# Attention and expert layer: stacked Q and K parts kept once in DRAM, reciprocals and statistics moved, top-2 late

## The reference

```
x = x + xattn(layernorm(x), ctx, ctx)     # 16 tiles of 128 rows, HD = 8 rows a head: 256 x 256 scores a head
x = x + ffn(layernorm(x))                 # gate: 2 of 8 experts a row, 256 -> 512 -> 256, silu(h0) * h1
qk = einsum('bdm,bdn->bmn', qh, kh) * 8 ** -0.5;  sm = softmax(qk);  ret = einsum('bmn,bcn->bcm', sm, vh)
```

## Time and profile before

| what | value |
|---|---|
| median of 3 runs | 544.45 us (544.16 to 548.63) |
| profiled execution | 544.45 us |
| its span | 542.7 us |
| TensorE, share of the span busy | 81% |
| VectorE | 52% |
| ScalarE | 42% |
| GpSimd | 40% |
| granted TensorE clock, mean | 0.898 |
| DMA in all | 69.91 MB, mean 129 GB/s |
| SyncE's DMA queue | 29698 packets, 41.37 MB |

### The profile page before, as it was taken

One profiled execution on the slowest core, in us unless ns is written; L12 is line 12 of the kernel. 1 busy time (PEld: TensorE's weight loads), 2 busy tenths in 40 slices (PEclk: granted clock), 3 DMA queues, 4 the chain that ended last, 5 costly groups with the idle time before them and its releaser, 6 DMA issues.

```text
span 542.7 us, 10122 instructions
## 1 busy us (share of the span) xinstructions
PE 439.4 (81%) x3150; PEld 228.9 (42%) x3151; DVE 283.7 (52%) x599; ACT 230.6 (42%) x456; POOL 216.0 (40%) x224
## 2 busy tenths in 40 slices
PE   0336789889897967999714899999999999999991
PEld 0301234234342423332312465665665665665660
DVE  7169887988888857964789122222222222222220
ACT  0302698686777764787400322222222222222220
POOL 3530703262626333333383134534444544544522
PEclk9955699898999997788955799999999999999996
DMA  5899547586776892537393022232232232232321
GB/s 183 200 302 280 167 118 197 168 229 185 217 211 187 245 276 92 200 103 248 109 383 105 30 40 39 42 54 39 40 56 39 42 55 39 41 56 39 41 38 19
DMA packets 45208, 69.91 MB, mean 129 GB/s; under 512 B 6887, under 2 KB 34200, under 8 KB 45176
## 3 DMA queue, kind: packets, MB, share of 16 engines
q1 hardware_dynamic: 29698, 41.37, 27.0%
q0 software_dynamic: 11424, 24.39, 19.8%
q10 hardware_dynamic: 4054, 3.72, 2.4%
HBM read 42.57 MB, written 26.58 MB: 127 GB/s over the span
## 4 chain that ended last, share of the span: by engine, by line
PE 53%; DMA 18%; DVE 13%; ACT 6%; SPq 6%; issue 2%; POOLq 0%; POOL 0%; DVEq 0%; ACTq 0%
PE max_ps L1379 25%; DMA den<-acc 7%; PE ring_ps L1389 6%; PE pv_ps L1389 6%; ACT pt L742 5%; PE pv_ps L1283 5%; DVE mx L888 5%; DMA acc<-pvs 4%; PE ring_ps L1362 3%; PE ring_ps L1266 3%; SPq L425 2%; DMA q_img<-qpart 2%; PE max_ps L1178 2%; PE ring_ps L1352 2%; SPq L371 2%
## 5 line engine op out<-in xcount | busy, mean ns | idle before, releaser
L888 DVE TENSOR_REDUCE mx<-max_ps 128x4 f32<-128x1024 f32 x128 | 150.3, 1216 | 29.8 <-PE max_ps L1178 29.5
L742 ACT ACTIVATE pt<-ring_ps 128x512 f32<-128x512 f32 x256 | 139.1, 598 | 48.5 <-PE ring_ps L1266 45.8
L1379 PE MATMUL max_ps<-w_sb,pt 128*128 x312 | 143.0, 602 | 0.9 <-ACT pt L813 0.9
L682 POOL DMA_INDIRECT out<-rb,sidx x39 | 62.1, 1591 | 119.3 <-DVE gidx L1126 55.4
L1150 DVE TENSOR_TENSOR pt<-pt,max_ps 128x512 f32<-128x512 f32 x39 | 26.8, 688 | 125.2 <-PE max_ps L1379 66.2
L1283 PE MATMUL pv_ps<-pt,w_sb 128*27 128x256 f32 (+2 forms) x1024 | 85.4, 419 | 1.4 <-ACT pt L742 0.6
L1178 PE MATMUL max_ps<-K,Q 48*128 48x256 bf16 x512 | 56.8, 306 | 33.1 <-DVE mx L888 24.7
L1379 PEld LDWEIGHTS max_ps<-w_sb,pt 128*128 128x128 f32 x312 | 57.2, 193 | 58.8 <-issue 58.8
L1266 PE MATMUL ring_ps<-Q,K 50*128 50x256 f16 x512 | 54.4, 294 | 14.2 <-ACT pt L742 12.9
L820 ACT ACTIVATE pt<-ring_ps 128x512 f32<-128x512 f32 x39 | 23.3, 597 | 71.5 <-PE ring_ps L1362 71.5
L674 POOL DMA_INDIRECT pt<-xrow,gidx x39 | 38.8, 996 | 28.5 <-issue 14.0
(11 more groups left out here) (161 smaller groups left out, 398.7 us busy)
## 6 DMA issues: line engine op xcount, KB each, us to landing
w_sb<-in_L_ffn_w_kernel POOLq DMA_DIRECT2D x16, 512.0 KB, 7.6
K<-k_img SPq DMA_DIRECT2D x16, 448.0 KB, 6.0
Q<-q_img SPq DMA_DIRECT2D x16, 448.0 KB, 7.2
q_img<-qpart SPq DMA_DIRECT2D x32, 192.0 KB, 3.9
k_img<-kpart SPq DMA_DIRECT2D x28, 192.0 KB, 3.8
wo_sb<-in_L_ffn_wo_kernel POOLq DMA_DIRECT2D x8, 512.0 KB, 9.2
acc<-pvs SPq DMA_DIRECT2D x7, 512.0 KB, 3.8
q_sb<-in_x SPq DMA_DIRECT2D x16, 128.0 KB, 4.8
```

Source lines behind the costliest of these rows:

```text
L682: g.indirect_dma_start(xacc, bass.IndirectOffsetOnAxis(ap=sidx[sl.par][:, 0:1], axis=0), y_sb[sl.par], None, compute_op=ALU.add).then_inc( ...
L742: a.activation(pt[:, (2 * i + h) % PTN, :, :], bank(key)[:, :, :], ACT.Exp, scale=SCALE).then_inc(ring_read, 1)
L888: v.tensor_reduce(mx[:, t % 2, :, :, p].rearrange("q mt h -> q h mt"), max_ps[n % 2][:, :, :, :], axis=AX.X, op=ALU.max).then_inc(max_read, 1)
L1379: last = nc.tensor.matmul(flat(max_ps[sl.par][:, bank_of]), lhsT=xT[sl.par][:, k * P:(k + 1) * P], rhs=weight(w, e, KC, k), start=(k == 0) ...
```

## The change

- `q_img` and `k_img` hold each part once. `store_stack` issues four DMAs a group. `load_qk` issues six: for each half of `K` 48 rows of 8 KB that read 24 rows twice, for each half and part of `Q` 24 rows of 8 KB that read 8 rows three times. The fills of the images go.
- All x tiles are loaded at the start, and their statistics and normalisations stand before the loop.
- `recip` moves from pair 2 to pair 6 of the odd tile, `rows_stats` from pair 4 to pair 7. In the odd tile SyncE does `store_stack` and `store_rows` before `store_rd` and `load_rb`.
- GpSimd splits Q before `residual_norm`; the weight loads w0 and half of wo move behind the residual 4. `x_last` is loaded in tile 12.
- The top-2 of tiles 0 to 7 is taken at once after the loop. The weights' share of `told` is made on VectorE after the token's, and its 32 matmuls (`slot_weights`) stand between the slots 0 and 1 of the experts.

```diff
-        q_img = nc.dram_tensor("q_img", [3, IMG, PAIRS * 2 * M], f16).ap()
-        k_img = nc.dram_tensor("k_img", [3, IMG, PAIRS * 2 * M], bf16).ap()
+        q_img = nc.dram_tensor("q_img", [3, 2, QPARTS, HD * PAIRS, 2 * M], f16).ap()
+        k_img = nc.dram_tensor("k_img", [3, 2, KPARTS, HD * PAIRS, 2 * M], bf16).ap()
...
                     for h in range(2):
-                        half = slice(64 * h, 64 * h + 64)
-                        for a in range(QPARTS):
-                            r = 64 * h + HR // 2 * a
-                            dst = img[g % 3, r:r + HR // 2].rearrange("(b d) (p n) -> (d p) b n", d=HD, p=PAIRS)
-                            if img is k_img:
-                                src = part[half].rearrange("r b u m -> r b (u m)")
-                            else:
-                                src = part[half, a:a + 1].rearrange("r o u m -> r o (u m)").broadcast_to([64, KPARTS, 2 * M])
-                            sp.dma_start(dst, src).then_inc(stack_out, 16)
+                        sp.dma_start(img[g % 3, h].rearrange("b r n -> r b n"),
+                                     part[64 * h:64 * h + 64].rearrange("r b u m -> r b (u m)")).then_inc(stack_out, 16)
...
-                for i in range(2):
-                    pairs = slice(PAIRS // 2 * i, PAIRS // 2 * (i + 1))
-                    n = slice(PAIRS * M * i, PAIRS * M * (i + 1))
-                    sp.dma_start(K[g % 3][0:IMG, pairs].rearrange("r p u m -> r (p u m)"), k_img[g % 3, :, n]).then_inc(qk_in[g % 3], 16)
-                    sp.dma_start(Q[g % 3][0:IMG, pairs].rearrange("r p u m -> r (p u m)"), q_img[g % 3, :, n]).then_inc(qk_in[g % 3], 16)
+                sp.wait_ge(stack_out, (g + 1) * 64)
+                for h in range(2):
+                    k_rows = k_img[g % 3, h].rearrange("b (d p) n -> (b d) (p n)", p=PAIRS)
+                    sp.dma_start(K[g % 3][64 * h:64 * h + HR].rearrange("r p u m -> r (p u m)"),
+                                 k_rows[None].broadcast_to([QPARTS, KPARTS * HD, PAIRS * 2 * M])).then_inc(qk_in[g % 3], 16)
+                for h in range(2):
+                    for i in range(QPARTS):
+                        r = 64 * h + HR // 2 * i
+                        q_rows = q_img[g % 3, h, i].rearrange("(d p) n -> d (p n)", p=PAIRS)
+                        sp.dma_start(Q[g % 3][r:r + HR // 2].rearrange("r p u m -> r (p u m)"),
+                                     q_rows[None].broadcast_to([KPARTS, HD, PAIRS * 2 * M])).then_inc(qk_in[g % 3], 16)
...
+                    if s + 3 < ST:
+                        store_stack(s + 3)
+                    if t >= 5:
+                        store_rows(s - 2)
                     if t >= 3:
                         store_rd(s - 1)
                         load_rb(s - 1)
-                    if t >= 5:
-                        store_rows(s - 2)
-                    if s + 3 < ST:
-                        store_stack(s + 3)
...
-                if t >= 3 and t % 2 == 1 and p == 2:
+                if t >= 3 and t % 2 == 1 and p == 6:
                     recip((t - 3) // 2)
-                if t >= 4 and t % 2 == 0 and p == 4:
+                if t >= 4 and t % 2 == 0 and p == 7:
                     rows_stats((t - 4) // 2)
-                if t >= 6 and t % 2 == 0 and p == 2:
-                    choose((t - 6) // 2)
...
+            def slot_weights():
+                pe.wait_ge(weights_done, TOPK * (PAY - 1))
+                for k in range(TOPK):
+                    for t in range(T):
+                        n = k * T + t
+                        last = nc.tensor.matmul(y_ps[1][:, 1, 0:(PAY - 1) * NT].rearrange("p (c i) -> p c i", c=PAY - 1),
+                                                lhsT=onehot_s[:, k, t, :], rhs=told[:, 1:PAY, k, t, :],
+                                                start=(n == 0), stop=(n == TOPK * T - 1))
+                last.then_inc(weights_full, 1)
```

More of the change, by code:

```diff
@@ L451, in _ @@
                 sp.dma_start(q_sb[:, t, :], tile_of(x, t)).then_inc(x_in[t // 2], 16)
+            for t in range(6, T):
+                sp.dma_start(q_sb[:, t, :], tile_of(x, t)).then_inc(x_in[t // 2], 16)
             store_stack(0, False)
@@ L759, in _ @@
             for k in range(3):
[L760 to L763, removed]
+                for h in range(2):
+                    r = 64 * h + HR
+                    a.dma_start(K[k][r:r + MXP].rearrange("r p u m -> r (p u m)"), kc[0:16, :]).then_inc(kc_in, 16)
             a.wait_ge(k_split, 1)
             for h in range(2):
[L766 to L769, removed]
+                a.dma_start(k_img[0, h].rearrange("b r n -> r b n"),
+                            kpart[64 * h:64 * h + 64].rearrange("r b u m -> r b (u m)")).then_inc(stack_out, 16)
             a.wait_ge(nbias_done, 1)
@@ L778, in _ @@
                 evac_v(m)
-            a.wait_ge(qk_in[0], 64)
+            a.wait_ge(nbias_done, 3)
+            for t in range(6, T):
+                normalise(t)
+            a.wait_ge(qk_in[0], 96)
             for t in range(6, T):
@@ L1013, in _ @@
                 then(v.memset(ends[i][:, 0:lead_e], 0.0))
-            choose(ST - 4)
-            count(ST - 4, range(T - 6))
+            choose(ST - 5, range(T - 8))
+            count(1, range(T - 8))
             recip(ST - 2)
@@ L1019, in _ @@
             stats_last([x2_last[:, 0, :]], 2)
-            choose(ST - 3)
-            count(ST - 3, unit_tiles[ST - 3])
+            choose(ST - 3, range(T - 8, T - 4))
+            count(2, range(T - 8, T - 4))
             v.wait_ge(num_in, (ST - 1) * 96)
@@ L1073, in _, with tell @@
             then(v.tensor_copy(slot_f[:, 0], slot_i[:, 1]))
-            def where(k):
-                return v.tensor_tensor(onehot_t[:, k], slot_f[:, 1, k, :, None].broadcast_to([P, T, NT]),
-                                       iota_t[:, None, :].broadcast_to([P, T, NT]), ALU.is_equal)
-            def tell(c):
-                then(v.tensor_tensor(told[:, c, 0], onehot_t[:, 0], pay[:, c, 0, :, None].broadcast_to([P, T, NT]), ALU.mult))
-            where(1).then_inc(onehot_done, 1)
-            v.wait_ge(norm_done, 1)
-            then(v.tensor_scalar(wts[:, 0, :], norm[:, :], WSCALE, None, ALU.mult))
-            then(v.tensor_tensor(wts[:, 1, :], wts[:, 0, :], e2[:, :], ALU.mult))
-            then(v.tensor_copy(pay[:, 1], wts[:, :, :]))
-            v.tensor_tensor(pay[:, 2], wts[:, :, :], pay[:, 1], ALU.subtract).then_inc(pay_done, 1)
-            then(where(0))
-            tell(0)
-            v.wait_ge(pay_done, 1)
-            tell(1)
-            tell(2)
+            for k in range(TOPK):
+                then(v.tensor_tensor(onehot_t[:, k], slot_f[:, 1, k, :, None].broadcast_to([P, T, NT]),
+                                     iota_t[:, None, :].broadcast_to([P, T, NT]), ALU.is_equal))
+            def tell(c, k):
+                return v.tensor_tensor(told[:, c, k], onehot_t[:, k], pay[:, c, k, :, None].broadcast_to([P, T, NT]), ALU.mult)
+            for k in range(TOPK):
+                then(tell(0, k))
             for k in range(TOPK):
@@ L1120, in _ @@
                                    op1=ALU.mult).then_inc(slots_done, 1)
+            v.wait_ge(norm_done, 1)
+            then(v.tensor_scalar(wts[:, 0, :], norm[:, :], WSCALE, None, ALU.mult))
+            then(v.tensor_tensor(wts[:, 1, :], wts[:, 0, :], e2[:, :], ALU.mult))
+            then(v.tensor_copy(pay[:, 1], wts[:, :, :]))
+            then(v.tensor_tensor(pay[:, 2], wts[:, :, :], pay[:, 1], ALU.subtract))
+            for k in range(TOPK):
+                for c in range(1, PAY):
+                    tell(c, k).then_inc(weights_done, 1)
             def next_gather(sl):
@@ L1150, in experts @@
                     v.tensor_tensor(inter[sl.par], sil[sl.par], flat(max_ps[sl.par][:, 1]), ALU.mult).then_inc(inter_done, 1)
+                if sl.peeled and sl.t == 1:
+                    v.wait_ge(weights_full, 1)
+                    then(v.tensor_copy(wlow[:, :], y_ps[1][:, 1, NT:2 * NT]))
+                    v.scalar_tensor_tensor(wslot[:, :], y_ps[1][:, 1, 0:NT], 1.0, wlow[:, :], op0=ALU.mult,
+                                           op1=ALU.add).then_inc(weights_read, 1)
+                    v.wait_ge(weights_read, 1)
+                    then(v.tensor_scalar(wslot[:, :], wslot[:, :], 1.0 / WSCALE, None, ALU.mult))
                 if sl.has(-1):
@@ L1384, in output @@
                 pe.wait_ge(interT_done, sl.t + 1)
+                if sl.peeled and sl.t == 1:
+                    pe.wait_ge(weights_read, 1)
                 if sl.has(-2):
@@ L1406, in experts @@
                     turn_x(sl.at(1))
+                if sl.peeled and sl.t == 0:
+                    slot_weights()
                 if sl.has(-1):
```

133 lines of the change are left out of this document (48 added, 85 removed).

## The result

The changed kernel takes 675.57 us (median of 4, 670.86 to 675.91) against 546.54 (544.16 to 549.01) for the kernel before on the same chip: ratio 1.234, 95% interval 1.225 to 1.243. The forecast was 642, in a range of 565 to 695. The profiled execution took 675.91 us with a span of 674.2. Ratios throughout leave out the few runs that lay more than 1.5% above the fastest of their kernel.

A forecast was written before the change was run, and what follows sets the result against it. K/Q loads on two or three DMA engines, with SyncE's queue behind them, were taken to bound the kernel: 544.5 + 104.8 (start and loop) - 1 - 3 - 2 = 643, said as 642 us, range 565 to 695.

The forecast's parts named there:

- Width of the loads: Six K/Q loads: the leading DRAM count limits the engines, 2 for a K load, 3 for Q, always the first ones.
- Rate: K/Q loads: 655 kB on each busiest engine, 23.8 us at 27.5 GB/s; 25.5 us taken, 27 from first issue to landing.
- Start: Before the loop: group 0 load ends at 45.4 us, first exp matmul 79.5 instead of 49.40, +30 us.
- the stop of tile 0: Tile 0, if the loads spread well: it loses its stop, -4 us.
- rival A: K/Q loads spread well over the engines, so the kernel takes 511 us; chance 0.16.
- Period: Loop: 40 us for two tiles instead of 27.6; `mrow` issue of tile 12 at 322 us, +104.8 with the start included.
- Behind the last load: Tiles 12 to 15 less 1 us; moved weight loads, late top-2 and early `x_last` -3, between -6 and +3.
- (-1, -3, -2): After the loop's loads: -1 for tiles 12 to 15, -3 for weight loads and top-2, -2 for routing.
- Routing: Between attention and experts: -4.4 from comparisons and products, 2.4 for the 32 small matmuls, net -2 us.
- the tail's 5: Behind the last load, counted in the 511 us case: -3 for weight loads and top-2, -2 for routing.
- B: K/Q loads: one of the two shapes spreads, the other does not, 562 to 570 us; chance 0.06.
- C: K/Q loads: an engine does 16.3 GB/s also when few run, 40 us a load, 758 us in all; chance 0.04.

The follow-up runs named there:

- the third run: The changed kernel with its images, but K in four plain loads of 24 rows and Q in twelve of 8 rows, no repeated dimension: 560.07 us, ratio 1.033.
- the first run: The changed kernel with the images, stores and loads of before, all its other moves kept: 522.76 us, ratio 0.960.
- the prologue undone: The changed kernel with the images of before and, put back besides, late x tiles, their statistics and normalisations in tiles 0 and 1: 531.17 us, 0.973.
- K once and Q three times: The changed kernel with K stored once, in four plain loads of 24 rows, and Q stored three times, in two of 48 rows: 524.88 us, ratio 0.963.

## Why the prediction was right, step by step

- **Width of the loads: right.** I read from one shape (`num`, 4 x 8 rows) that the leading count limits the engines. The window at 40 us shows 2.1 engines, the third run takes the repeat away and 115 us with it.
- **Rate: a little high, and in part luck.** I divided the 110 GB/s of the window by four engines, though its share of 0.33 counts 5.3; by those it is 20.8 GB/s each. Two engines give 24.5, between the two. For 655 kB that is 26.7 us instead of 23.8; my 25.5 had part of it. Issue to matmul was 29.3 for 27 in group 0, and `den`, next in the queue, arrived 31.4 us after K's first issue in tile 2 (the reciprocal starts at 154.60), as this row of VectorE's timeline of the changed kernel shows:

```profile
154.60 0.55 DVE L913 RECIPROCAL rd<-den 128x64 f32<-128x64 f32 x1 [15.51 <-DMA den<-acc]
```

- **Start: right.** First score matmul 46.50 for 45.4, first exp matmul 79.98 for 79.5, tile 2 at 114.98 for 115.5. Statistics and normalisations cost nothing under the wait, as said; on fast loads they are a gain of 7 us, against the 4 for the stop of tile 0 in rival A.
- **Period: the step that was short.** Between the `mrow` issues 121.21 and 340.63 lie five periods of 43.9 us; I said 40. From K's first issue to the exp matmul of the next even tile it is 35.0 (123.15 to 158.14) instead of 27 + 4.5 = 31.5. The 8.3 from there to the next issue are right (the issues of `mrow` and `acc`, 1.4 and 0.4 behind my 6.5; the 190.33 - 187.06 that I named is 3.3 and would have given more): 158.14 to 166.30, as this row of SyncE's timeline of the changed kernel shows:

```profile
166.30 1.30 SPq L370 DMA_DIRECT2D K<-k_img  x2
```

  Five times 3.9, less 0.8 at the start (121.21 for 122), is the 18.6 us by which the issue of tile 12 stands behind my 322. The cause is the load and what is queued behind it, 3.5 us longer than I took them, not the blocked issues: in the run on ScalarE's queue `den` and `num` are issued freely and the period is 42.5.
- **Behind the last load: wrong sign.** I said -6 in all (-1, -3, -2); from the `mrow` issue of tile 12 to the end it is 333.6 us for 325.5 before, +8.1. The issue of tile 13 at 357.19 meets eight weight loads of 512 KB, and TensorE waits 13 us. GpSimd's and TensorE's timelines and the window of the changed kernel:

```profile
352.88 2.95 POOL L591 DMA_DIRECT2D w_sb<-in_L_ffn_w_kernel  x4
355.83 2.99 POOL L604 DMA_DIRECT2D wo_sb<-in_L_ffn_wo_kernel  x4
...
376.88 1.26 POOL L524 TENSOR_TENSOR num<-num,rb 128x512 f32<-128x512 f32 x1 [18.06 <-DMA rb<-rden]
```

```profile
372.83 0.61 PE L1238 MATMUL ring_ps<-Q,K 50*128 50x256 f16 x4 [13.01 <-DMA Q<-mrow]
```

```profile
358.00:370.00 12.00, 1.82 (x24) 0.88 (x20) 2.89 (x5) 2.09 (x5) 0.82 (x2) 0.71 1.02 335
```

  I had named `rb` as what the batch might meet, with +3 as the end; it met `mrow` as well. In the first run the `mrow` of tile 13 is issued at 207.57, just ahead of the second part of the batch at 208.39, and TensorE waits 2 us in all. There the stretch is 325.8 us: no gain either. What the batch does hangs on tenths of a microsecond: with the prologue undone `mrow` is issued at 213.59 and the batch at 214.10, and TensorE waits 11.15 us.
- **Routing: right, a little small.** The four products and comparisons take 3.3 us instead of 7.7, as said. The 32 matmuls on the path, which I took at 2.4, are 1.32 us. From the first expert matmul to the end it is 242.6 us (431.61 to 674.2) for 242.4 before. By these parts the routing gives some 4 us, not 2; no run has it alone, and the run that keeps only it, the late top-2 and the late weights gains 0.3% in all, under 2 us. VectorE's and TensorE's timelines of the changed kernel:

```profile
416.89 1.65 DVE L1046 TENSOR_TENSOR q_sb<-slot_f,iota_t 128x624 f16<-128x624 f32 x2
418.58 1.65 DVE L1050 TENSOR_TENSOR q_sb<-q_sb,pay 128x624 f16<-128x624 f16 x2
```

```profile
436.86 1.32 PE L1339 MATMUL ring_ps<-q_sb,K 128*128 128x78 f16 x32
```

  With the top-2 late and the rest undone the `mrow` issue of tile 12 comes at 211.31 instead of 217.19, 5.9 us earlier, but the stretch from there to the end is 328.0 for 325.5: what the top-2 frees in the loop comes back in part behind it.
- **Rivals.** A is what the kernel becomes with wide loads; I had put it at 511, and it is 522.8, since the loop gives 13 and not 18 to 20, and nothing is left of the tail's 5. B had the range 562 to 570 for one shape alone narrow; K alone narrow gives 634.8. B was priced too low: it left out that Q's wide loads put 96 KB on the same two engines, so 480 KB, 20 us by 24.5 GB/s, not the 14, and the queue comes on top. Q alone narrow was not run. C, 16.3 GB/s an engine, is excluded by the 24.5.

The sum, in the span: 322 + 319.5 = 641.5 as forecast, +18.6 for the period and the start, +14.1 for the stretch behind (333.6 for the 319.5 of my sum), is the 674.2 of the profiled execution. The mechanism was right; its price was some 33 us too low, for the period and for the stretch behind the last load.

## What to carry to other kernels

Look at what a load's access patterns begin with before counting its bytes. Saving DRAM bytes by a repeated leading dimension of 2 or 3 put the whole load on two or three DMA engines; here a load of a seventh fewer bytes (1.5 MB for 1.75) took 29.3 us instead of 9.4. A load also holds up what is queued behind it: the small transfers (`den`, `mrow`) inherit its time. So multiply its length by the number of times that one of them is on the path, and take that as an upper bound: eight loads were on the path here, and each us of load was worth 6 us of time, not 8 (40.8 us for 6.7).

The version to keep is the change with the images and loads of before: 522.8 us, against 544.4 before and 675.6.

## What the runs showed of the hardware that I had not expected

- SyncE's own issues block when the queue behind few engines is long. Four `den` issues took 10.19 us and four `num` issues 11.60 (2.61 and 2.49 in the earlier trace rows); two issues of `k_img` stores at 23.70 us took 7.62. In the run where ScalarE had the loads SyncE issued `den` and `num` in 2.63 and 2.52 us, though the `mrow` behind them took 3.81; ScalarE's own four Q issues took 3.19 us there and stood ahead of exps.
- An `mrow` of two transfers of 8 KB, issued amid a batch of 4 MB that GpSimd issues from 352.88 to 358.82, arrived 15.6 us later (357.19 to 372.83), at 335 GB/s on all engines: here another queue was no way past a full set of engines.
- An engine of the pair moved some 24.5 GB/s (51 over 2.1), against 12.6 to 20.9 when nearly all 16 ran (192 over 15.2 in the window of K once and Q three times, 260 over 16, 335 over 16 above). With few engines each was faster, but by far less than their number fell.
